# Result stores issued by ScalarE, fewer landing waits on GpSimd's indirect transfers, and separate buffers for the last gathers, in a six-layer attention and mixture-of-experts kernel

## The chip, the cores and the metric

The kernel runs on one core of a Trainium2 chip, in one launch. The metric is the device time of that launch in microseconds (us). The core has TensorE (PE), VectorE (DVE), ScalarE (ACT) and GpSimd (POOL); SyncE (SP) only issues DMAs. ScalarE can issue DMAs too, on a queue of its own. GpSimd issues the indirect ones, which scatter or gather rows by a list of indices.

## The reference

The input is 4096 tokens of 128 numbers (16 batches of 256), and six layers are applied one after another, each to the layernorm of the running sum `x`.

```
x = x + 0.5 * moe0(ln(x))      # 8 experts, top 1, hidden 512, relu squared
x = x + attn0(ln(x))           # latent attention, 8 heads
x = x + 0.5 * moe0(ln(x))
x = x + 0.5 * moe1(ln(x))      # 32 experts, top 4 + a shared expert, hidden 128, silu gate
x = x + attn1(ln(x))           # rotary attention, 16 heads of 8
x = x + 0.5 * moe1(ln(x))
```

In a mixture-of-experts layer each token goes to its K best experts only (K = 1 in moe0, 4 in moe1), and the K outputs are added up with the router's weights.

## The kernel before

Work is ordered by semaphores that are written by hand; each engine runs its own program in order. The names with `rt_`, `dp_`, `bl_`, `cb_` and `sh_` are semaphores. `x` stays in SBUF (`X`), as 32 tiles of 128 tokens; four tiles are a group, so there are 8 groups (0 to 7). Code calls the two kinds of layer `L0` ("top1", moe0) and `L1` ("top4", moe1).

A mixture-of-experts layer has two parts, of 16 tiles each, and these stages:

1. Routing (`route_vector`): VectorE works out for each token and choice a row in a table of slots in HBM, sorted by expert, into `ROW`.
2. Sending (`dispatch_pool`, line 619): GpSimd scatters the normed tokens to `L.xs` (shown as slots_top), one indirect transfer of 128 rows (64 KB) for each tile and choice: 64 for each part in L1, 16 in L0. It waits now and then until all that it has sent has landed (`dp_sent`), in L1 once in 8 transfers in the first part and once in 4 in the second, in L0 never in the first part and once in 4 in the second. Meanwhile PE, ACT and DVE work on the first half of the shared expert (L1 only).
3. Blocks: a step takes four blocks of 128 slots (L1; two in L0), each with its expert's weights. A part has 24 steps in L1 and 12 in L0. SyncE (`blocks_sync`) loads step s+3 (line 764) into one of four buffers `XG` once the transposes of step s are done, and stores the results of step s-2 (L1; s-1 in L0) from one of two buffers `YS` to `L.ys` (results_top, line 768). Step s of PE (`top4_tensor`) is: transposes of step s+1 (line 887), up of s (902), down of s-2 (924), transposes of the hidden values of s-1 (910). ACT copies the transposed inputs (959), applies silu (969) and copies the result of s-2 into `YS` (953), in this order. The first loads wait for the first part's sending, and the load of step 24, part 2's first, waits for all of part 2's sending. So the results of steps 22 and 23 are made only after step 24's load, in PE's steps 24 and 25.
4. Gathering (`combine_pool`, line 1075): when all results of a part are stored (`bl_st`), GpSimd gathers them back, group by group, 16 transfers of 128 rows each in L1 (4 in L0). In L1 group g goes to half g % 2 of a buffer `YG`, once VectorE has combined group g-2 (`cb_add`). It waits for landing after every 4 transfers in groups 0 to 3, and after the first 8 only in groups 4 to 7.
5. Combining (`combine_group`, line 1096): VectorE adds the gathered rows to `X`, groups 0 to 2 between the block steps of part 2 (after its steps 11, 17 and 23), group 3 after them, and groups 4 to 7 in a tail in which PE, ACT and VectorE also do the second half of the shared expert (`TAIL`) and the next layer's layernorm. The shared expert uses the second half of `HF[:, 0]` for a turned copy.

## Time and profile before

| | |
|---|---|
| median of 3 runs | 1943.48 us (1939.62 to 1945.4) |
| profiled execution, its own time | 1943.49 us |
| its span in the trace | 1941.6 us |
| busy: PE, DVE, ACT, POOL | 63%, 58%, 40%, 50% of the span |
| the two moe1 layers in the trace | sending begins at 635.19 and 1506.52 us; the last group's combine begins at 1056.98 and 1927.81 us |

The span runs from the first to the last instruction; 1.9 us of the execution's own time lie around it. Busy shares are averages over stages with different limits. A row of the timeline gives start and length in us, and in brackets how long the engine was idle before it and who ended that; "issue" is time in which it waited for nothing that the profile shows.

### The profile page before, as it was taken

The numbers are of one execution on the slowest core, as the hardware profiler recorded it, in microseconds if no ns is written. First come the engines' busy times: TensorE is split into PE (matmuls) and PEld (weight loads), VectorE is DVE, ScalarE is ACT, GpSimd is POOL, SyncE is SP. The second block draws the span as 40 slices with busy tenths as digits, with TensorE's granted clock in tenths as the row PEclk, the third lists the DMA queues.
The fourth block names the chain that finished last, engine by engine and source line by source line (L and its number), as shares of the span: only waits on it lengthen the run. The fifth ranks groups of instructions, "written<-read, shape, count | busy, mean of one in ns | idle before, by whom it ended". The sixth has DMA issues, their size and how long they took to land.

```text
span 1941.6 us, 34590 instructions
## 1 busy us (share of the span) xinstructions
PE 1223.6 (63%) x11544; PEld 904.9 (47%) x11545; DVE 1135.1 (58%) x2883; ACT 782.2 (40%) x1164; POOL 966.6 (50%) x1052
## 2 busy tenths in 40 slices
PE   2397587862981359779353578777762349678360
PEld 1297355551981128668321244444432129678320
DVE  6546667666468713225357699899978713225332
ACT  2153266650440114334111488788881114334110
POOL 0625145443241665535574467666740665535564
PEclk9998689985995589889776555555555679889785
DMA  8233044401220115345211000000000115345212
GB/s 336 66 96 103 18 155 148 139 15 37 87 82 14 41 46 179 130 137 167 83 49 35 13 2 2 2 2 2 2 2 1 43 58 177 122 147 160 78 49 76
DMA packets 99997, 150.42 MB, mean 77 GB/s; under 512 B 21408, under 2 KB 54816, under 8 KB 99104
## 3 DMA queue, kind: packets, MB, share of 16 engines
q1 hardware_dynamic: 79392, 106.76, 16.7%
q0 software_dynamic: 20480, 41.98, 7.4%
q8 instruction: 79, 1.29, 0.3%
q14 instruction: 46, 0.38, 0.1%
HBM read 74.16 MB, written 74.45 MB: 77 GB/s over the span
## 4 chain that ended last, share of the span: by engine, by line
POOL 24%; PE 23%; issue 16%; DMA 15%; DVE 14%; SPq 5%; ACT 2%; DVEq 0%; ACTq 0%; POOLq 0%
POOL slots_top L619 12%; POOL AREA L1075 11%; DMA slots_top<-XN,ROW 6%; DMA AREA<-results_top,ROW 5%; PE PS L841 4%; SPq L1274 3%; PE PS L293 2%; PE PS L295 2%; PE PS L294 2%; PE PS L1718 2%; DVE AREA L1884 2%; PE PS L1734 2%; PE PS L1706 2%; DMA query_rows<-AREA 1%; PE PS L412 1%
## 5 line engine op out<-in xcount | busy, mean ns | idle before, releaser
L619 POOL DMA_INDIRECT slots_top<-XN,ROW x320 | 315.0, 984 | 363.2 <-DVE ROW L573 183.8
L1075 POOL DMA_INDIRECT AREA<-results_top,ROW x320 | 305.2, 954 | 310.9 <-DMA results_top<-AREA 123.6
L990 DVE SCALAR_TENSOR_TENSOR AREA<-PS,AREA 128x512 f32<-128x512 f32 x96 | 66.4, 691 | 295.5 <-ACT AREA L969 295.0
L1679 POOL TENSOR_TENSOR AREA<-AREA 128x1024 f16<-128x1024 f32 x64 | 151.3, 2364 | 91.1 <-ACT AREA L1819 90.9
L902 PE MATMUL PS<-WGU,AREA 128*128 x768 | 189.5, 391 | 0.0
L1908 DVE TENSOR_REDUCE AREA<-PS 128x4 f32<-128x1024 f32 x128 | 156.0, 1219 | 30.1 <-PE PS L1706 29.3
L1812 ACT ACTIVATE AREA<-PS,AREA 128x1024 f32<-128x1024 f32 x128 | 142.7, 1115 | 52.6 <-PE PS L1718 52.4
L902 PEld LDWEIGHTS PS<-WGU,AREA 128*128 128x128 f32 x768 | 144.0, 198 | 17.1 <-ACT AREA L959 0.4
L1307 POOL TENSOR_TENSOR AREA<-AREA 128x1536 f16<-128x1536 f32 x32 | 92.9, 2904 | 98.4 <-ACT AREA L1522 98.4
L1819 ACT ACTIVATE AREA<-AREA 128x1024 f16<-128x1024 f32 x128 | 135.5, 1059 | 0.0
L412 PE MATMUL PS<-IDF,XN 128*128 128x128 f32 x192 | 50.4, 422 | 135.0 <-DVE XN L402 135.0
L1096 DVE SCALAR_TENSOR_TENSOR X<-AREA,W,X 128x128 f32<-128x128 f32 x256 | 73.2, 348 | 93.3 <-DMA AREA<-results_top,ROW 91.5
L887 PE MATMUL PS<-IDF,AREA 128*128 128x128 f32 x384 | 61.2, 286 | 102.0 <-DMA AREA<-slots_top 102.0
L1734 PEld LDWEIGHTS PS<-AREA 128*128 128x128 f16 x1024 | 63.2, 105 | 124.9 <-issue 84.6
L1734 PE MATMUL PS<-AREA 128*128 (+1 forms) x1024 | 75.2, 179 | 69.3 <-ACT AREA L1840 35.4
L924 PE MATMUL PS<-WD,AREA 128*128 x768 | 103.8, 279 | 12.9 <-DVE AREA L985 12.9
L924 PEld LDWEIGHTS PS<-WD,AREA 128*128 128x128 f32 x768 | 102.0, 194 | 20.3 <-DVE AREA L985 11.8
L959 ACT ACTIVATE AREA<-PS 128x512 f32<-128x512 f32 x96 | 57.3, 597 | 130.3 <-PE PS L887 123.7
L705 ACT ACTIVATE AREA<-PS 128x512 f32<-128x512 f32 x64 | 38.2, 597 | 173.9 <-PE PS L295 173.8
L969 ACT ACTIVATE AREA<-PS 128x512 f32<-128x512 f32 x96 | 57.5, 599 | 122.7 <-PE PS L902 110.9
L412 PEld LDWEIGHTS PS<-IDF,XN 128*128 128x128 f32 x192 | 33.7, 212 | 143.0 <-DVE XN L402 103.0
L1884 DVE TENSOR_TENSOR AREA<-AREA 128x1024 f16<-128x1024 f32 x64 | 97.1, 1517 | 3.4 <-ACT AREA L1819 3.3
(260 smaller groups left out, 3558.9 us busy)
## 6 DMA issues: line engine op xcount, KB each, us to landing
AREA<-slots_top SPq DMA_DIRECT2D x96, 256.0 KB, 3.0
results_top<-AREA SPq DMA_DIRECT2D x96, 256.0 KB, 2.1
slots_top<-ZERO SPq DMA_DIRECT2D x24, 512.0 KB, 3.1
AREA<-slots_top SPq DMA_DIRECT2D x48, 128.0 KB, 2.3
results_top<-AREA SPq DMA_DIRECT2D x48, 128.0 KB, 1.7
AREA<-query_rows SPq DMA_DIRECT2D x48, 128.0 KB, 2.9
slots_top<-XN,ROW POOLq DMA_INDIRECT x320, 2.2
AREA<-results_top,ROW POOLq DMA_INDIRECT x320
```

The source lines that it names most:

```text
L412: ins = nc.tensor.transpose(banks(at + g % 2)[:, j * P:(j + 1) * P], XN[:, t * D:(t + 1) * D], IDF[:, :])
L619: nc.gpsimd.indirect_dma_start(out=L.xs[q], out_offset=bass.IndirectOffsetOnAxis(ap=ROW[:, n:n + 1], axis=0), in_=XN[:, t * D:(t + 1) * D] ...
L902: ins = nc.tensor.matmul(o, XTF[:, v, j * P:(j + 1) * P], w, start=True, stop=True)
L924: ins = nc.tensor.matmul(banks(6 + v)[:, j * D:(j + 1) * D], HF[:, v, 4 * P + j * P:4 * P + (j + 1) * P], w, start=True, stop=True)
L1075: nc.gpsimd.indirect_dma_start(out=YG[:, at:at + D], out_offset=None, in_=L.ys[g * GT // L.tiles], in_offset=bass.IndirectOffsetOnAxis(ap= ...
L1307: nc.gpsimd.tensor_tensor(PB0[1][:, u % 2, :], PF[:, u % 2, :], PB0[0][:, u % 2, :], ALU.subtract).then_inc(a_plo.sem, 1)
L1679: nc.gpsimd.tensor_tensor(PB1[1][:, g, :], PF1[:, g, :], PB1[0][:, g, :], ALU.subtract).then_inc(b_plo[1].sem, 1)
L1734: nc.tensor.matmul(banks(6)[:, o:o + 17], p[0], v, start=k == 0, stop=False)
L1812: nc.scalar.activation(PF1[:, g, :], banks(4, 2), ACT.Exp, bias=LNSP[:, 0:1], scale=SCALE1).then_inc(b_exp.sem, 1)
L1819: nc.scalar.activation(PB1[0][:, g, :], PF1[:, g, :], ACT.Copy).then_inc(b_phi.sem, 1)
L1884: nc.vector.tensor_tensor(PB1[1][:, g, :], PF1[:, g, :], PB1[0][:, g, :], ALU.subtract).then_inc(b_plo[0].sem, 1)
L1908: nc.vector.reduce_max(by_group(MX[:, c % 2, :], g), PS[:, 2:4, :].rearrange("p b (r k) -> p b r k", k=256), axis=AX.X).then_inc(b_max.sem, 1)
```

## The change

It has four pieces. Results are stored from ScalarE's queue, directly behind the copy that makes them (`store_result`), and SyncE only loads. GpSimd's waits for landing in L1 become rarer: once in 16 transfers in the first part of sending and once in 8 in the second, and in gathers of groups 0 to 3 once in 8. In L1 groups 6 and 7 are gathered into the space of `XG` and `HF`, which are free when the blocks are done, in place of the halves of `YG`. The shared expert's turned copy moves from `HF` to `XTF`, so that it doesn't meet group 7. L0 keeps its four buffers and its waits.

```diff
-        self.ring = 4 if K == 1 else 2
+        self.slot = [g % 4 for g in range(NG)] if K == 1 else [0, 1, 0, 1, 0, 1, 2, 3]
+        self.turn = [self.slot[:g].count(u) for g, u in enumerate(self.slot)]
...
+        turned_rows = XTF[:, 0, :]
+        slots = {"top1": [YG[:, u * GT * D:(u + 1) * GT * D] for u in range(4)],
+                 "top4": [YG[:, :GT * 4 * D], YG[:, GT * 4 * D:], XG.rearrange("p a b -> p (a b)"),
+                          HF.rearrange("p a b -> p (a b)")]}
...
-                every = 4 if q > 0 else 8 if L is L1 else 0
+                every = (16, 8)[q] if L is L1 else (0, 4)[q]
                 if every and n % every == every - 1:
                     pool.wait_ge(*dp_sent[q].at(16 * (n % (L.tiles * L.K) + 1)))
...
-                nc.scalar.activation(HF[:, 0, GC:2 * GC], banks(4), ACT.Copy).then_inc(sh_tc.sem, 1)
+                nc.scalar.activation(turned_rows, banks(4), ACT.Copy).then_inc(sh_tc.sem, 1)
...
-                if not is_static(s) or s >= behind:
-                    store(s - behind, (u - behind) % 4)
...
-            for s in range(L.steps - behind, L.steps):
-                store(s, s % 4)
+            sp.wait_ge(*bl_y.at(L.steps))
+
+        def store_result(act, L, s, u, q):
+
+            act.wait_ge(*bl_y.at(s + 1))
+            rows = L.ys[q].rearrange("(n p j) c -> p n (j c)", p=P, j=L.J)
+            nc.scalar.dma_start(rows[:, bass.ds(s - q * L.part_steps, 1), :].rearrange("p a c -> p (a c)"),
+                                YS[:, u % 2, :L.J * D]).then_inc(bl_st[u % 2].sem, 16)
...
                 nc.scalar.activation(YS[:, u % 2, :], banks(6 + u % 2), ACT.Copy).then_inc(bl_y.sem, 1)
+                store_result(act, L, s, u, s // L.part_steps if is_static(s) else part[0])
...
-                u = g % L.ring
-                wait(pool, cb_add[u], g // L.ring)
+                u = L.slot[g]
+                wait(pool, cb_add[u], L.turn[g])
...
-                    if c % 4 == 3 and (g < NG // 2 or c % 8 == 7 and c < GK - 1):
-                        pool.wait_ge(*cb_got[u].at(16 * (g // L.ring * GK + c + 1)))
+                    if c % 8 == 7 and (g < NG // 2 or c < GK - 1) or L is L0 and c == 3 and g < NG // 2:
+                        pool.wait_ge(*cb_got[u].at(16 * (L.turn[g] * GK + c + 1)))
```

GpSimd's program at the end of the second part's sending and the beginning of the gathers of moe1 was this before (a row is a run of equal instructions; what the first of them waits for stands in brackets, and the semaphores are "dispatched", "block_stored", "combine_gathered" and "combine_added"):

```order
L619 DMA slots_top4_1<-XN,ROW 12288x128 [waits dispatched1]
L619 DMA slots_top4_1<-XN,ROW 12288x128 x3
L1075 DMA AREA<-results_top4_0,ROW 128x128 [waits block_stored1,block_stored,dispatched1]
L1075 DMA AREA<-results_top4_0,ROW 128x128 x3
L1075 DMA AREA<-results_top4_0,ROW 128x128 [waits combine_gathered0]
```

The same place in the changed program:

```order
L624 DMA slots_top4_1<-XN,ROW 12288x128 [waits dispatched1]
L624 DMA slots_top4_1<-XN,ROW 12288x128 x7
L1086 DMA AREA<-results_top4_0,ROW 128x128 [waits block_stored1,block_stored,dispatched1]
L1086 DMA AREA<-results_top4_0,ROW 128x128 x7
L1086 DMA AREA<-results_top4_0,ROW 128x128 [waits combine_gathered0]
```

Runs of four became runs of eight, sending and gathering; what the first gather waits for is the same.

The gathers of groups 5 to 7, in GpSimd's program of before:

```order
L1075 DMA AREA<-results_top4_1,ROW 128x128 [waits combine_added1]
L1075 DMA AREA<-results_top4_1,ROW 128x128 x7
L1075 DMA AREA<-results_top4_1,ROW 128x128 [waits combine_gathered1]
L1075 DMA AREA<-results_top4_1,ROW 128x128 x7
L1075 DMA AREA<-results_top4_1,ROW 128x128 [waits combine_added0]
```

And now:

```order
L1086 DMA AREA<-results_top4_1,ROW 128x128 [waits combine_added1]
L1086 DMA AREA<-results_top4_1,ROW 128x128 x7
L1086 DMA AREA<-results_top4_1,ROW 128x128 [waits combine_gathered1]
L1086 DMA AREA<-results_top4_1,ROW 128x128 x15
L1086 DMA AREA<-results_top4_1,ROW 128x128 [waits combine_gathered2]
```

Group 6 follows group 5 with no wait for VectorE's combine of group 4 between them; the wait after eight transfers of a group is still there.

## Rows read from the trace of the kernel before

**Rows 1.** The page: the span, and each engine's busy time, share and instructions.

```profile
span 1941.6 us, 34590 instructions
PE 1223.6 (63%) x11544; PEld 904.9 (47%) x11545; DVE 1135.1 (58%) x2883; ACT 782.2 (40%) x1164; POOL 966.6 (50%) x1052
```

**Rows 2.** The page: the chain that ended last, shares by line.

```profile
POOL slots_top L619 12%; POOL AREA L1075 11%; DMA slots_top<-XN,ROW 6%; DMA AREA<-results_top,ROW 5%; PE PS L841 4%; SPq L1274 3%; PE PS L293 2%; PE PS L295 2%; PE PS L294 2%; PE PS L1718 2%; DVE AREA L1884 2%; PE PS L1734 2%; PE PS L1706 2%; DMA query_rows<-AREA 1%; PE PS L412 1%
```

**Rows 3.** Timeline of GpSimd, first moe1 layer: where its stages begin.

```profile
635.19 1.00 POOL L619 DMA_INDIRECT slots_top<-XN,ROW  x1 [41.25 <-DVE ROW L573]
...
727.40 0.96 POOL L619 DMA_INDIRECT slots_top<-XN,ROW  x1 [1.54 <-DMA slots_top<-XN,ROW]
...
855.30 0.97 POOL L1075 DMA_INDIRECT AREA<-results_top,ROW  x1 [20.40 <-DMA results_top<-AREA]
...
967.18 0.94 POOL L1075 DMA_INDIRECT AREA<-results_top,ROW  x1 [1.81 <-DMA AREA<-results_top,ROW]
```

**Rows 4.** Timeline of SyncE's queue, first moe1 layer: part 2's first load.

```profile
836.19 0.33 SPq L764 DMA_DIRECT2D AREA<-slots_top  x1
836.57 0.43 SPq L768 DMA_DIRECT2D results_top<-AREA  x1
```

**Rows 5.** Timeline of PE, first moe1 layer: the transposes of step 24.

```profile
839.06 1.12 PE L887 MATMUL PS<-IDF,AREA 128*128 128x128 f32 x4 [27.89 <-DMA AREA<-slots_top]
```

**Rows 6.** GpSimd's waits (total us, times, longest): 635:728, 728.5:806, 806.5:836, 856.5:936, 936:968.

```profile
POOL slots_top L619 <- DMA slots_top<-XN,ROW: 12.3, 8, 1.5
...
POOL slots_top L619 <- DMA slots_top<-XN,ROW: 25.4, 11, 2.8
...
POOL slots_top L619 <- DMA slots_top<-XN,ROW: 6.1, 4, 1.5
...
POOL AREA L1075 <- DMA AREA<-results_top,ROW: 27.2, 11, 3.2
...
POOL AREA L1075 <- DMA AREA<-results_top,ROW: 9.1, 5, 1.9
```

**Rows 7.** The same view in the last layer: stretches 1600:1708 and 1727:1838.5.

```profile
POOL slots_top L619 <- DMA slots_top<-XN,ROW: 30.9, 15, 2.9
...
POOL AREA L1075 <- DMA AREA<-results_top,ROW: 36.5, 16, 2.9
```

**Rows 8.** GpSimd's groups of instructions, 727.3:836: busy us, mean ns, idle before.

```profile
L619 POOL DMA_INDIRECT slots_top<-XN,ROW x64 | 61.4, 959 | 47.7 <-DMA slots_top<-XN,ROW 33.1 <-issue 14.6
```

**Rows 9.** Timeline of GpSimd: a stall, and waits behind 20 and 16 transfers.

```profile
63.94 5.49 POOL L619 DMA_INDIRECT slots_top<-XN,ROW  x1 [0.30 <-issue]
...
487.48 0.95 POOL L619 DMA_INDIRECT slots_top<-XN,ROW  x1 [1.79 <-DMA slots_top<-XN,ROW]
...
1000.41 0.94 POOL L1075 DMA_INDIRECT AREA<-results_top,ROW  x1 [1.81 <-DMA AREA<-results_top,ROW]
```

**Rows 10.** Timeline of VectorE: combines of groups 0, 2, 3 and 7, then the last layer's last.

```profile
887.75 4.65 DVE L1096 SCALAR_TENSOR_TENSOR X<-AREA,W,X 128x128 f32<-128x128 f32 x16
...
940.87 4.68 DVE L1096 SCALAR_TENSOR_TENSOR X<-AREA,W,X 128x128 f32<-128x128 f32 x16 [2.94 <-DMA AREA<-results_top,ROW]
945.58 0.87 DVE L366 BATCH_NORM_STATS2 STAT<-X 128x6 f32<-128x128 f32 x4
...
966.94 4.69 DVE L1096 SCALAR_TENSOR_TENSOR X<-AREA,W,X 128x128 f32<-128x128 f32 x16 [20.49 <-DMA AREA<-results_top,ROW]
...
1056.98 4.67 DVE L1096 SCALAR_TENSOR_TENSOR X<-AREA,W,X 128x128 f32<-128x128 f32 x16 [0.87 <-DMA AREA<-results_top,ROW]
...
1927.81 4.66 DVE L1096 SCALAR_TENSOR_TENSOR X<-AREA,W,X 128x128 f32<-128x128 f32 x16 [18.25 <-DMA AREA<-results_top,ROW]
```

**Rows 11.** Timeline of ACT: a step of L0's blocks and one of L1's.

```profile
521.74 1.02 ACT L1021 ACTIVATE AREA<-PS 128x1024 f32<-128x1024 f32 x1 [0.67 <-PE PS L295]
...
854.37 0.60 ACT L969 ACTIVATE AREA<-PS 128x512 f32<-128x512 f32 x1 [1.13 <-PE PS L902]
```

**Rows 12.** The page: a result store of L1, KB each and us to landing.

```profile
results_top<-AREA SPq DMA_DIRECT2D x96, 256.0 KB, 2.1
```

More of the change, by code:

```diff
@@ L660, in turned @@
                 for t in range(GT):
-                    ins = nc.tensor.transpose(banks(7)[:, t * D:(t + 1) * D], HF[:, 0, GC + t * P:GC + (t + 1) * P],
+                    ins = nc.tensor.transpose(banks(7)[:, t * D:(t + 1) * D], turned_rows[:, t * P:(t + 1) * P],
                                               IDF[:, :])
@@ L752, in blocks_sync, with of_step @@
             sp.wait_ge(*dp_sent[0].at(16 * L.tiles * L.K))
-            XC, YC = L.J * D, L.J * D
-            def of_step(parts, s):
+            XC = L.J * D
+            def of_step(s):
                 q = s // L.part_steps if is_static(s) else part[0]
-                rows = parts[q].rearrange("(n p j) c -> p n (j c)", p=P, j=L.J)
+                rows = L.xs[q].rearrange("(n p j) c -> p n (j c)", p=P, j=L.J)
                 return rows[:, bass.ds(s - q * L.part_steps, 1), :].rearrange("p a c -> p (a c)")
             part = [0]
-            behind = 2 if L is L1 else 1
             def load(s, u):
-                sp.dma_start(XG[:, u, :XC], of_step(L.xs, s)).then_inc(bl_load[u].sem, 16)
-            def store(s, u):
-                sp.wait_ge(*bl_y.at(s + 1))
-                sp.dma_start(of_step(L.ys, s), YS[:, u % 2, :YC]).then_inc(bl_st[u % 2].sem, 16)
+                sp.dma_start(XG[:, u, :XC], of_step(s)).then_inc(bl_load[u].sem, 16)
             def step(s, u):
@@ L953, in result @@
                 nc.scalar.activation(YS[:, u % 2, :], banks(6 + u % 2), ACT.Copy).then_inc(bl_y.sem, 1)
+                store_result(act, L, s, u, s // L.part_steps if is_static(s) else part[0])
+            part = [0]
             def x_copy(s, u):
@@ L973, in top4_scalar @@
             x_copy(0, 0)
-            stepped(act, 0, L.steps, step)
+            for q in range(L.parts):
+                part[0] = q
+                stepped(act, q * L.part_steps, (q + 1) * L.part_steps, step)
             result(L.steps - 2, 2)
@@ L1012, in result @@
                                      ).then_inc(bl_y.sem, 1)
+                store_result(act, L, s, u, s // L.part_steps if is_static(s) else part[0])
+            part = [0]
             def step(s, u):
@@ L1025, in blocks_scalar @@
             x_hi(0, 0)
-            stepped(act, 0, L.steps, step)
+            for q in range(L.parts):
+                part[0] = q
+                stepped(act, q * L.part_steps, (q + 1) * L.part_steps, step)
             result(L.steps - 1, 3)
@@ L1070, in combine_pool @@
                         pool.wait_ge(*bl_st[u].at(8 * L.part_steps * (g * GT // L.tiles + 1)))
-                u = g % L.ring
-                wait(pool, cb_add[u], g // L.ring)
+                u = L.slot[g]
+                wait(pool, cb_add[u], L.turn[g])
                 for c in range(GK):
-                    at = (u * GK + c) * D
                     nc.gpsimd.indirect_dma_start(
-                        out=YG[:, at:at + D], out_offset=None, in_=L.ys[g * GT // L.tiles],
+                        out=slots[L.tag][u][:, c * D:(c + 1) * D], out_offset=None, in_=L.ys[g * GT // L.tiles],
                         in_offset=bass.IndirectOffsetOnAxis(ap=ROW[:, g * GK + c:g * GK + c + 1], axis=0)
                     ).then_inc(cb_got[u].sem, 16)
-                    if c % 4 == 3 and (g < NG // 2 or c % 8 == 7 and c < GK - 1):
-                        pool.wait_ge(*cb_got[u].at(16 * (g // L.ring * GK + c + 1)))
+                    if c % 8 == 7 and (g < NG // 2 or c < GK - 1) or L is L0 and c == 3 and g < NG // 2:
+                        pool.wait_ge(*cb_got[u].at(16 * (L.turn[g] * GK + c + 1)))
         def combine_group(dve, L, g, last):
-            u, GK = g % L.ring, GT * L.K
-            dve.wait_ge(*cb_got[u].at((g // L.ring + 1) * (16 * GK)))
-            y = YG[:, u * GK * D:(u + 1) * GK * D]
+            u, GK = L.slot[g], GT * L.K
+            dve.wait_ge(*cb_got[u].at((L.turn[g] + 1) * (16 * GK)))
+            y = slots[L.tag][u]
             if L.K == 1:
@@ L1103, in combine_group @@
             if not last:
-                dve.wait_ge(*cb_add[u].at(g // L.ring + 1))
+                dve.wait_ge(*cb_add[u].at(L.turn[g] + 1))
                 for j in range(GT):
@@ L1958, in moe_counts @@
                 c.update({bl_st[u]: 8 * L.steps})
-            for u in range(L.ring):
-                c.update({cb_got[u]: 16 * GT * L.K * (NG // L.ring), cb_add[u]: NG // L.ring})
+            for u in range(4):
+                c.update({cb_got[u]: 16 * GT * L.K * L.slot.count(u), cb_add[u]: L.slot.count(u)})
             for u in range(4):
@@ L1992, in each_phase @@
                 if ph in ("moe0", "moe1"):
-                    ready = [(cb_add[u].sem, cb_add[u].base) for u in range(2)]
+                    ready = [(cb_add[u].sem, cb_add[u].base) for u in range(4)]
                     if n + 1 < len(phases):
```

## Prediction

> **What bounds the kernel now.** I read the busy times first: no engine is busy for more than 63% of the span, and GpSimd for 50% [rows 1], so the answer lies in who waits for whom. The chain that ended last names GpSimd's sends and gathers for 23% of the span and the landing of just these transfers for 11% more, far ahead of any other line [rows 2]. So I followed GpSimd through the first moe1 layer. It sends part 1 from 635.19 us, part 2 from 727.40, gathers from 855.30, and begins the gathers of group 4 at 967.18 [rows 3]. Each of these beginnings but the gathers' waits only for its own earlier transfers to land. The one at 855.30 waited 20.40 us for result stores. Why: SyncE issues the load of step 24 at 836.19, when part 2's sending has landed [rows 4]; PE had stood still for 27.89 us before it got this data at 839.06 [rows 5]; and the results of steps 22 and 23 need three more steps. So the path is GpSimd's sending, then 855.30 - 836.19 = 19.1 us of blocks, then GpSimd's gathering, and the block work of part 1 and the rest of part 2 lie beside it.
>
> The tail follows. The combine of group 3 begins at 966.94 and that of group 7 at 1056.98, with only 0.87 us of waiting for a gather before it [rows 10], so VectorE's own chain and GpSimd's gathers take the same 90 us there. In the last layer, which prepares no layernorm, the last combine had waited 18.25 us for its gather [rows 10]: there GpSimd alone sets the end.
>
> **The waits for landing.** A send takes 0.96 us and the next begins 0.30 us later; 64 of them take 61.4 + 47.7 us with their waits, of which 14.6 us are the 48 ordinary gaps [rows 8]. A wait for landing stands in place of such a gap, so it costs its length less 0.30. In five stretches [rows 6]:
> - part 1's sending: 12.3 / 8 = 1.54, so 1.24 us each;
> - part 2's sending beside block work: 25.4 / 11 = 2.31, so 2.01 each; after the blocks stopped: 6.1 / 4 = 1.53, so 1.23 each;
> - gathers beside block work: 27.2 / 11 = 2.47, so 2.17 each; after it: 9.1 / 5 = 1.82, so 1.52 each.
>
> The question is whether a wait behind 8 or 16 transfers is longer than one behind 4 or 8. The nearest rows: behind 20 unwaited sends in moe0 the wait was 1.79, behind 16 unwaited gathers 1.81 [rows 9], against 1.53 and 1.82 behind four in quiet stretches. So in quiet it is a latency, paid once whatever the number. Beside block work only waits behind four are shown. I take the same 2.31 and 2.47, as they are 0.77 and 0.65 above the quiet ones, which block traffic explains without a backlog; the other two values are in the rivals.
>
> **The sum, first moe1 layer.**
> 1. Part 1's sending: 8 waits become 4. 4 x 1.24 = 5.0 us. The blocks begin that much earlier, and so does part 2's sending, at 722.4.
> 2. Part 2's sending: the 15 waits inside it become 7, the last landing stays. Eight sends and a wait take 8 x 1.26 + 2.01 = 12.1 us, so the seventh wait ends near 807. Part 1's blocks stop at 839.06 - 27.89 - 5.0 = 806.2, so all seven are beside block work. Gain (11 x 2.01 + 4 x 1.23) - 7 x 2.01 = 13.0 us. Part 2's first load is issued at 836.2 - 18.0 = 818.2; PE still waits for it, some 15 us instead of 27.89, so no new bound appears.
> 3. The gathers then begin 18.0 us earlier, at 837.3. Groups 0 to 3 have 8 waits instead of 16. Eight gathers and a wait take about 8 x 1.25 + 2.17 = 12.2 us; the block part ends 18 us earlier too, which puts six of the waits beside it and two behind. Gain (11 x 2.17 + 5 x 1.52) - (6 x 2.17 + 2 x 1.52) = 31.5 - 16.1 = 15.4 us.
> 4. Group 3's combine can then begin at 966.94 - 33.4 = 933.5. VectorE is ready for it: it was ready for group 2's combine at 940.87 - 2.94 = 937.9, now at 919.9, and with that combine and its statistics done (4.68 + 0.87 us) it is ready for group 3 at 925.5. The buffers hold: group 2's gathers begin near 886, and the combine of group 0, which frees their half, began at 887.75, so now at 869.8, with 4.65 us of work [rows 10].
> 5. The tail keeps its waits (one behind eight transfers in each group), its gathers and VectorE's chain: 0.
> Together 33.4 us.
>
> **Last layer.** The same code and nearly the same rows: 30.9 us for 15 waits where the first has 31.5, and 36.5 for 16 where it has 36.3 [rows 7]. 5.0 + 12.7 + 15.5 = 33.2 us.
>
> **The pieces that I cost at nothing.**
> - Stores on ScalarE's queue. In SyncE's order the store issued at 836.57 stood behind the load that waited for part 2's sending [rows 4], but the next result that would need its buffer is made only behind that load's transposes, so nobody waited. The results of steps 22 and 23, for which the gathers wait, stay bound to step 24. What is added is a wait for ACT's own copy and an issue of 0.33 to 0.43 us [rows 4] in each step, with the input copy and silu (in L0 relu) queued behind. ACT had stood idle for 1.13 us before silu and 0.67 us before relu [rows 11], which covers 0.5. If the cover is gone, an issue costs at most 0.43 on each of 144 steps, 62 us; but blocks are on the path only in L0's two layers (48 steps, 21 us) and for some three steps of each moe1. The Trainium skill says (DMA: Bandwidth & Descriptors, "Issuing engines are not separate DMA queues") that DMAs started by several engines end on the same 16 DMA engines and save only issue time; a gain here would contradict it, and the sum has none.
> - Own rooms for groups 6 and 7. They take away the wait for the combines of groups 4 and 5. The gathers of group 6 begin some 43 us behind 967.18, and group 4's combine is done by then: in the 90 us of the tail GpSimd's stops are for its own landings, as the 1.81 at 1000.41 [rows 9]. 0 us.
> - The turned copy in another place, and two more semaphores at the end: the same instructions, 0.
>
> Sum: 1943.5 - 33.4 - 33.2 = 1876.9 us. It is made against the profiled execution's 1943.49 (span 1941.6, plus 1.9 around it), which is the median of the three runs, 1943.48.
>
> **Rivals.**
> - *Waits grow with what is in flight.* For it: beside block work even four transfers wait longer. If the part above the quiet wait doubles (0.77 for 7 and 0.65 for 6 waits in each layer), 2 x (5.4 + 3.9) = 18.6 us are lost: 1895.5. If the time beside block work stays wholly what it was, what remains is per layer 5.0 + 4 x 1.23 + 3 x 1.52 = 14.5: 1914.5. Against it: the quiet rows behind 16 and 20. Chance 0.19, mostly the first. The Trainium skill speaks for it: DMA: Bandwidth & Descriptors ("Latency and other measured facts") puts HBM's access latency at 0.2 us on average and 2 us at high load; by that each of 26 waits could be 1.8 us longer, an estimate of 47 us and 1924. The rows have shown 0.77 at most.
> - *Waits shrink.* Before, the rhythm of four gathers and a wait (about 7 us) was close to two block steps, so a wait could meet a load each time. With another rhythm all 26 may come down to the quiet ones: 18.6 us more gain, 1858.3. VectorE's readiness (4.) allows some 8 us more per layer, just so much. Chance 0.08.
> - *ACT is held by its DMA.* If ACT's queue stood until a store lands (2.1 us [rows 12]), it would be over its cover by about 1 us per step, mostly off the path in moe1, and add 20 to 50 us: 1900 to 1930. Chance 0.04.
> - *Slower: GpSimd itself stalls when more than eight of its transfers are out.* One send of 640 took 5.49 us in place of 0.96, and it was the ninth of a sequence with no wait [rows 9]. If each of the 4 + 8 + 8 groups of a layer met such a stall once, 40 x 4.5 = 180 us come back: 2057. It decides against the change from 66.6 / 40 = 1.7 us per group on. Against it: the twenty sends before 487.48 and the sixteen gathers before 1000.41 ran with no such stall. Chance 0.03.
> - *No change*: the path's waits are replaced by others, say PE's blocks, to within 0.3%. PE's 27.89 us of standing still speak against it. Chance 0.03.
>
> My forecast with its own range, 1867 to 1887, has 0.63. The range from 1858 to 1900 takes in the shrinking waits and the doubled ones. Faster by over 0.3% (a bound that I take as what a measurement here can tell from no change): 0.94; within it 0.03; slower 0.03.
>
> **What would show it.** In the changed profile: a wait behind 16 sends of about 1.5 us, and four of them; part 2's first load about 183 us behind the first send (201 before); GpSimd's waits beside block work near 2.3 and 2.5 us, half as many; PE's stop before step 24 near 15 us; the first gather about 19 us behind that load, and group 3's combine about 298 us behind the first send (332 before); a tail of 90 us; block steps as long as before. I am wrong if the waits that are left are much longer, if a stall inside a send appears, if block steps become longer with ACT's issues in them, or if VectorE comes late to group 3.

## Result: 1872.1 us for 1941.6, and the opposite on two other chips

Timed beside the kernel before on one chip, the changed kernel took 1872.09 us (median of four runs, 1870.31 to 1873.8), the kernel before 1941.55 (1938.97 to 1945.4). The ratio is 0.9641, with a 95% interval of 0.9625 to 0.9657: faster by 3.6%. The forecast sum of 1876.9 was 4.8 us too high, and the time lies in the narrow range, 1867 to 1887. The experiments below show that this holds for some chips only: on two others the changed kernel and all its variants with rarer waits are 6 to 10% slower than the kernel before (the variant with the old waits: 1.3%). No step of the prediction speaks of that.

The profile's page of the changed kernel: its span, the engines' busy times, and the chain that ended last by engine and by line. Line 619 of before is now 624 (the sends), 1075 is 1086 (the gathers), 1096 is 1107 (the combines).

```profile
span 1872.0 us, 34469 instructions
...
PE 1221.8 (65%) x11513; PEld 902.4 (48%) x11545; DVE 1135.0 (61%) x2883; ACT 785.3 (42%) x1164; POOL 968.9 (52%) x1052
...
PE 33%; POOL 19%; DVE 18%; issue 14%; DMA 8%; SPq 4%; ACT 2%; DVEq 0%; ACTq 0%; another core or an unknown queue 0%; POOLq 0%
POOL slots_top L624 14%; POOL AREA L1086 5%; PE PS L845 4%; PE PS L906 4%; DMA slots_top<-XN,ROW 3%; PE PS L298 3%; SPq L1285 3%; DVE X L1107 3%; PE PS L300 3%; PE PS L299 3%; PE PS L1729 2%; PE PS L928 2%; DVE AREA L1895 2%; PE PS L1745 2%; PE PS L1717 2%
```

Against [rows 1] and [rows 2] no engine's busy time moved by more than about 3 us. What went is waiting: the landing of sends has 3% of the chain where it had 6%, and the landing of gathers, 5% before, is no longer in the list. The chain now goes through PE's blocks and VectorE's combines instead of through GpSimd's gathers, which had 11% and have 5%.

GpSimd's stages in the first moe1 layer, from its timeline (start, duration, then the idle time before and what ended it), beside [rows 3]:

```profile
640.64 1.00 POOL L624 DMA_INDIRECT slots_top<-XN,ROW  x1 [41.26 <-DVE ROW L578]
...
729.21 0.96 POOL L624 DMA_INDIRECT slots_top<-XN,ROW  x1 [1.54 <-DMA slots_top<-XN,ROW]
...
840.26 0.97 POOL L1086 DMA_INDIRECT AREA<-results_top,ROW  x1 [19.57 <-DMA results_top<-AREA]
...
935.56 0.94 POOL L1086 DMA_INDIRECT AREA<-results_top,ROW  x1 [1.89 <-DMA AREA<-results_top,ROW]
```

Part 1's sending takes 88.6 us (92.2 before), part 2's and the blocks behind it 111.1 (127.9), the gathers of groups 0 to 3 95.3 (111.9). From the first send to the first gather it is 199.6 us for 220.1, and to group 4's gathers 294.9 for 332.0.

GpSimd's waits in the stretches 640.6:730, 730:841 and 841:935 of the first moe1 layer and in its tail, 935:1030 (total us, times, longest), beside [rows 6]:

```profile
POOL slots_top L624 <- DMA slots_top<-XN,ROW: 6.2, 4, 1.5
...
POOL slots_top L624 <- DMA slots_top<-XN,ROW: 14.7, 8, 2.5
...
POOL AREA L1086 <- DMA AREA<-results_top,ROW: 13.9, 6, 3.0
POOL AREA L1086 <- DVE X L1107: 2.1, 2, 1.8
...
POOL AREA L1086 <- DMA AREA<-results_top,ROW: 9.4, 5, 1.9
```

Four waits of 1.54 us behind 16 sends each, as forecast. The eight of the second row are the seven inside part 2's sending and once more the 1.54 before it: 13.2 / 7 = 1.88 us where waits behind four sends had been 2.31 beside block work. (In the last layer the seven are 14.3 us, 2.04 each.) Nowhere does a wait show a backlog. The Trainium skill (DMA: Bandwidth & Descriptors, "Latency and other measured facts") puts HBM's access latency at 2 us at high load, which stood behind the estimate of 1924 us. Whether the load here is high in its sense, no run shows; the waits beside block work are on average 0.3 and 0.5 us above the quiet 1.54 in the two layers, not 1.8 (the longest single one is 3.3).

The row for VectorE names no wait for a combine. It holds one gap of 0.30 and this one, the first of the two rows:

```profile
900.42 0.94 POOL L1086 DMA_INDIRECT AREA<-results_top,ROW  x1 [1.77 <-DVE X L1107]
...
911.86 0.94 POOL L1086 DMA_INDIRECT AREA<-results_top,ROW  x1 [1.76 <-DMA AREA<-results_top,ROW]
```

900.42 is the sixth run of eight, the second half of group 2. There GpSimd's program waits for landing only; the wait for group 1's combine stands before group 3, at 911.86. The trace's landing events say the same: the last transfer of the run before landed at 900.17. Group 1's combine happened to end at 895.73 + 4.66 = 900.39, so the view names it. All eight waits of groups 0 to 3 are for landing, 17.5 us together.

PE, SyncE's queue and VectorE at the places of [rows 4], [rows 5] and [rows 10], from their timelines: PE's transposes of step 24, the loads from part 2's first one on, and the combines of groups 1, 3 and 7, and the last layer's last.

```profile
824.65 1.12 PE L891 MATMUL PS<-IDF,AREA 128*128 128x128 f32 x4 [11.85 <-DMA AREA<-slots_top]
...
821.97 4.16 SPq L768 DMA_DIRECT2D AREA<-slots_top  x5
...
895.73 4.66 DVE L1107 SCALAR_TENSOR_TENSOR X<-AREA,W,X 128x128 f32<-128x128 f32 x16
...
935.33 4.68 DVE L1107 SCALAR_TENSOR_TENSOR X<-AREA,W,X 128x128 f32<-128x128 f32 x16 [9.06 <-DMA AREA<-results_top,ROW]
...
1023.59 4.66 DVE L1107 SCALAR_TENSOR_TENSOR X<-AREA,W,X 128x128 f32<-128x128 f32 x16
...
1858.16 4.67 DVE L1107 SCALAR_TENSOR_TENSOR X<-AREA,W,X 128x128 f32<-128x128 f32 x16 [16.28 <-DMA AREA<-results_top,ROW]
```

Group 3's combine comes 935.33 - 640.64 = 294.7 us behind the first send (331.75 before), group 7's 382.95 (421.8). The last combine of this layer no longer waits for its gather: VectorE's chain ends the layer now. (In the last layer it still waits, 16.28 us.)

The tail is 935.33 to 1023.59, 88.3 us, where it was 90.0. In the kernel before GpSimd made one stop there that the changed kernel, with rooms of their own for groups 6 and 7, does not have. It is behind group 7's first gather, and the profile gives no reason:

```profile
1032.17 0.95 POOL L1075 DMA_INDIRECT AREA<-results_top,ROW  x1 [0.30 <-issue]
1035.27 0.95 POOL L1075 DMA_INDIRECT AREA<-results_top,ROW  x1 [2.16 <-issue]
```

And ScalarE, which issues the stores now (L788), in one step of L1's blocks, beside [rows 11]:

```profile
840.15 0.60 ACT L957 ACTIVATE AREA<-PS 128x512 f32<-128x512 f32 x1 [0.29 <-PE PS L928]
840.78 0.34 ACTq L788 DMA_DIRECT2D results_top<-AREA  x1
841.22 0.60 ACT L965 ACTIVATE AREA<-PS 128x512 f32<-128x512 f32 x1 [0.47 <-PE PS L891]
842.75 0.60 ACT L975 ACTIVATE AREA<-PS 128x512 f32<-128x512 f32 x1 [0.94 <-PE PS L906]
843.64 0.60 ACT L957 ACTIVATE AREA<-PS 128x512 f32<-128x512 f32 x1 [0.29 <-PE PS L928]
```

The issue takes 0.34 us and fits into a gap in which ScalarE waits for PE. A step still takes 843.64 - 840.15 = 3.49 us.

Sum over the trace: 1941.6 - 1872.0 = 69.6 us. The first moe1 layer gives 38.8 up to group 7's combine, the last layer, from its first send at 1473.46 (1506.52 before) to the end, 36.5. Ahead of the first moe1, 5.5 us are lost (635.19 against 640.64), mostly in attn0, where nothing was changed. Two later experiments (f1 and f2) with the changed kernel's code up to there begin at 635.92 and 635.28, so it is not the code. Whether the other three executions of the changed kernel had it too is not known: they took 1.6 to 3.5 us less than the profiled one.

### The profile page after: what moved, and what is told of

It is laid out like the page before. It is cut to its first block, busy times and chain, and to the rows that moved or that the text cites. A ratio compares the mean times of both kernels' runs of the same rounds, so it can differ in the third digit from the quotient of the medians.

```text
span 1872.0 us, 34469 instructions
## 1 busy us (share of the span) xinstructions
PE 1221.8 (65%) x11513; PEld 902.4 (48%) x11545; DVE 1135.0 (61%) x2883; ACT 785.3 (42%) x1164; POOL 968.9 (52%) x1052
## 4 chain that ended last, share of the span: by engine, by line
PE 33%; POOL 19%; DVE 18%; issue 14%; DMA 8%; SPq 4%; ACT 2%; DVEq 0%; ACTq 0%; another core or an unknown queue 0%; POOLq 0%
POOL slots_top L624 14%; POOL AREA L1086 5%; PE PS L845 4%; PE PS L906 4%; DMA slots_top<-XN,ROW 3%; PE PS L298 3%; SPq L1285 3%; DVE X L1107 3%; PE PS L300 3%; PE PS L299 3%; PE PS L1729 2%; PE PS L928 2%; DVE AREA L1895 2%; PE PS L1745 2%; PE PS L1717 2%
## 5 line engine op out<-in xcount | busy, mean ns | idle before, releaser
L965 ACT ACTIVATE AREA<-PS 128x512 f32<-128x512 f32 x96 | 57.3, 597 | 131.0 <-PE PS L891 130.3
L710 ACT ACTIVATE AREA<-PS 128x512 f32<-128x512 f32 x64 | 38.2, 597 | 148.5 <-PE PS L300 147.6
L423 ACT ACTIVATE XT<-PS 128x512 f16<-128x512 f32 x48 | 28.7, 597 | 165.9 <-PE PS L417 165.9
```

## Experiments

There are twelve experiments, on four chips: A (e1 to e4), B (c1 to c3 and e5), C (f1 to f3) and D (g1). The kernel before was timed between the others on each chip, and the ratios below are to that. Among the twelve are both kernels unchanged (c1, c2) and one variant twice (e2, c3). The kernel before took 2003.59 us on A, 2006.25 on B, 1940.53 on C and 1941.84 on D. On C and D it has the time of the first comparison.

### First four, on chip A: which part gives the gain?

Theory A was the prediction's, that the waits alone give the gain; theory B that stores and rooms are needed for it. **e1_old_waits** is the changed kernel with the old waits:

```diff
-                every = (16, 8)[q] if L is L1 else (0, 4)[q]
+                every = 4 if q > 0 else 8 if L is L1 else 0
...
-                    if c % 8 == 7 and (g < NG // 2 or c < GK - 1) or L is L0 and c == 3 and g < NG // 2:
+                    if c % 4 == 3 and (g < NG // 2 or c % 8 == 7 and c < GK - 1):
```

> The changed kernel with the landing waits of before (8 and 4 sends, 4 gathers), but with ScalarE's stores and the own rooms kept. Theory A (the whole gain is the removed waits; stores and rooms are worth nothing): the time of before, 1941.5 us, within 4. Theory B (a queue of their own for the stores shortens the waits beside block work, as the profile of the changed kernel has them at 1.9 to 2.0 us in sending and 2.2 in gathering where before had 2.31 and 2.47): 22 waits in each moe1 layer shorter by some 0.35 us, 1926 us.

**e2_waits_only** is the kernel before with the two lines above turned the other way (stores on SP, shared rooms).

> The kernel before with the new, rarer waits alone; stores stay on SyncE's queue, two halves of YG, turned copy in HF. Theory A: the time of the changed kernel, 1872 us, within 4. Theory B: the waits beside block work go back to 2.31 and 2.47 us, 13 of them in each moe1 layer, so 1881 us.

**e3_no_rooms** is the changed kernel with the rooms and the turned copy as before:

```diff
-        self.slot = [g % 4 for g in range(NG)] if K == 1 else [0, 1, 0, 1, 0, 1, 2, 3]
+        self.slot = [g % 4 for g in range(NG)] if K == 1 else [0, 1, 0, 1, 0, 1, 0, 1]
...
-        turned_rows = XTF[:, 0, :]
+        turned_rows = HF[:, 0, GC:2 * GC]
```

> The changed kernel without the own rooms: groups 6 and 7 are gathered into the two halves of YG again and the turned copy is in HF. If the rooms are worth nothing: 1872 us, and no wait of GpSimd for VectorE in the tail. Rival (the rooms gave the tail, which is 1.8 us shorter in the first moe1 layer, its gain): 1875 to 1877 us.

**e4_first_send_8** is the changed kernel with `every = (8, 8)[q]` in place of `(16, 8)[q]`.

> The changed kernel with a wait once in 8 in the first part of sending, as before. Four more waits of 1.54 us in each moe1 layer, each in place of a gap of 0.30: 4 x 1.24 x 2 = 9.9 us more, 1882 us. Rival (the blocks, not GpSimd, set when things go on, so that these waits are hidden): 1872 us.

Measured on A: e1 2030.44 us, 1.0133 (1.0085 to 1.0181); e2 2192.98, 1.0959 (1.0897 to 1.102); e3 2198.34, 1.0991 (1.0935 to 1.1046); e4 2167.84, 1.0828 (1.078 to 1.0876). Theories A and B and the rivals beside them missed: here rare waits make the kernel 8 to 10% slower. The intervals of e2 and e3 overlap, and the two differ in the stores' queue alone, so it makes no difference that shows beside that.

### Next four, on chip B: is it the kernels or the chip?

**c1_after** is the changed kernel itself, **c2_before** the kernel before, **c3_waits_only** is e2 again.

> The changed kernel itself, beside the kernel before on one chip, because the first four experiments ran on a chip on which the kernel before took 2003.6 us instead of 1941.6 and every version with the rare waits was 8 to 10 per cent slower. Theory C (the chip decides: on some chips PE, ScalarE and VectorE stand still while GpSimd's transfers run without pauses): on a chip where the kernel before takes about 1942 us this takes 0.964 of it, as in the first comparison; on one where it takes about 2000 us, 1.08 to 1.10 of it, and the shared expert of the first group ends behind part 2's sending instead of ahead of it. Theory D (the experiments' kernels differ from the changed kernel in something that costs the 9 per cent): 0.964 on either chip.

> The kernel before, for its profile on this chip. Theory C: if its time is about 1942 us, the page is that of the profile before, with the shared expert's first group done about 72 us behind the first sending's start (706.8 for 635.2); if it is about 2000 us, the idle time that no core of this program explains shows on ScalarE and PE during the sendings here too, 30 to 60 us of it, and the rare waits only multiply it. Theory D: no such idle time on any chip.

> The kernel before with the rare waits alone: stores stay on SP's queue and the last gathers in the shared rooms. On the first chip it took 1.0959 of the time before. Theory A (the waits alone give the gain, where the chip lets them): 0.964 to 0.967 on a chip with about 1942 us. Theory B (stores on ScalarE's queue and own rooms are needed, since gathers would then wait for results or rooms): 0.975 to 0.99. On a chip with about 2000 us: 1.08 to 1.10 by theory C.

**e5_gather_4** is the changed kernel with the second edit of e1 alone, the gathers' wait.

> The changed kernel with the wait of the gathers of groups 0 to 3 back at once in 4 transfers. By the prediction's term (3), 15.4 us a layer of the second kind, 30.8 in all: 1903 us, or 0.980 of the time before, on a chip with about 1942 us. Rival: the gathers' gain was already lost to group 3's gathers waiting for the combine of group 1 (3.03, 1.77 and 2.37 us rows of the profile after), so that half of the term at most comes back: 1888 us, 0.972. On a chip with about 2000 us: if the dense gathers are what stalls the other engines, it comes down from 1.09 to 1.04 or less; if it is the sendings, it stays within 1 per cent of the changed kernel.

Measured on B: c1 2174.24 us, 1.084 (1.0794 to 1.0886); c2 2005.01; c3 2149.23, 1.0738 (1.068 to 1.0796); e5 2132.18, 1.0631 (1.0588 to 1.0674). The changed kernel, unchanged, is 8.4% slower than before here. (e5's rival rests on the 1.77 us taken for a wait for a combine; it is one for landing, as shown above.) So it is the chip, or what surrounds it (what else ran near it is not known), and not the experiments' code. The gathers' waits give 2% of the time back (e5, 1.063 for 1.084). With the sendings' waits back too (e1, on A) it is 1.013, so most of the rest goes with the sendings, if A and B are alike. Stores and rooms seem to cost about 1% there: e1 on A is 1.3% slower with the old waits, and c1 is 1% above c3, though their intervals just touch.

Where it goes: the page of c1_after, the chain by engine, then the same row of c2_before.

```profile
PE 33%; DVE 20%; another core or an unknown queue 20%; issue 14%; ACT 4%; SPq 4%; DMA 2%; POOL 1%; ACTq 1%; DVEq 0%; POOLq 0%
```

```profile
PE 22%; issue 19%; DVE 17%; POOL 16%; DMA 13%; another core or an unknown queue 5%; SPq 4%; ACT 3%; DVEq 0%; ACTq 0%; POOLq 0%
```

A fifth of the changed kernel's span is time in which an engine waited and no event in the profile explains its release. The program runs on one core, so the label ("remote" in the views of waits) only means "not known". On the first chip that share was 0%. GpSimd, by contrast, has 1% of the chain. Its stages on B, from the timelines of c1_after and then c2_before: first send and first gather, then the last layer's first send.

```profile
675.66 1.00 POOL L624 DMA_INDIRECT slots_top<-XN,ROW  x1 [43.77 <-DVE ROW L578]
...
952.89 0.97 POOL L1086 DMA_INDIRECT AREA<-results_top,ROW  x1 [99.09 <-DMA results_top<-AREA]
...
1666.44 1.04 POOL L624 DMA_INDIRECT slots_top<-XN,ROW  x1 [53.16 <-DVE ROW L578]
```

```profile
671.29 1.00 POOL L619 DMA_INDIRECT slots_top<-XN,ROW  x1 [44.03 <-DVE ROW L573]
...
891.97 0.97 POOL L1075 DMA_INDIRECT AREA<-results_top,ROW  x1 [19.45 <-DMA results_top<-AREA]
...
1561.86 1.04 POOL L619 DMA_INDIRECT slots_top<-XN,ROW  x1 [53.18 <-DVE ROW L573]
```

From first send to first gather it is 277.2 us against 220.7, and from there to the next moe1 713.6 against 669.9. GpSimd itself sends without being held up (part 1 takes 89.0 us, 88.6 on the first chip), and then stands still for 99 us, waiting for result stores of blocks that come late. Its landing waits while sending (677:850 in c1_after; total, times, longest) are all quiet ones:

```profile
POOL slots_top L624 <- DMA slots_top<-XN,ROW: 16.9, 11, 1.5
```

The others are late. First ScalarE's waits for its silu of the shared expert in c1_after (620:960, the same columns), then PE, ScalarE and VectorE at one such place, from their timelines:

```profile
ACT AREA L710 <- remote: 117.6, 10, 27.4
```

```profile
754.12 0.63 PE L300 MATMUL PS<-XT,SU 128*128 128x512 f16 x1
...
778.65 0.60 ACT L710 ACTIVATE AREA<-PS 128x512 f32<-128x512 f32 x1 [27.42 <-remote]
...
779.27 0.69 DVE L740 SCALAR_TENSOR_TENSOR AREA<-PS,AREA 128x512 f32<-128x512 f32 x1 [27.32 <-ACT AREA L710]
...
779.78 1.11 PE L666 MATMUL PS<-IDF,AREA 128*128 128x128 f32 x4 [25.03 <-issue]
```

PE's last product for this silu ended at 754.75 by the trace; ScalarE, whose other condition (VectorE's product before) had long been met, began at 778.65, 23.9 us late. VectorE followed as soon as ScalarE was done (0.02 us), and so did PE, which needed ScalarE's next copy (779.14 to 779.73). In the changed kernel on the first chip the same hand-over takes 0.03 us (PE ended at 678.67, ScalarE began at 678.70). So it is the hand-over from PE that comes late. Whether PE tells of its end late, or ScalarE learns of it or acts late, the trace does not say. Ten such waits, 117.6 us together, stand in the first moe1, all begun while GpSimd sends; the two before this one were late by 8.5 us (PE ended at 735.12, ScalarE began at 743.63) and 2.9 us (747.75, 750.63). PE's products are slower there too, 0.63 us for 0.38 on the first chip: the granted clock is 0.64 in 728:755 of c1_after and 0.95 in 674:680 of the first trace. That is PE at the lower of its two levels (1.2 and 2.4 GHz) after it has stood still, and 0.25 us a product does not explain a gap of 23.9. How late the shared expert's first half becomes (its last ScalarE instruction, counted from the first send) goes with the waits:

```
kernel, chip              waits in sendings   last ScalarE instr.   first gather
before, first chip        1 in 8 and 4         +70.3 us             +220.1 us
c2_before, B              1 in 8 and 4         +75.9                +220.7
e1_old_waits, A           1 in 8 and 4         +85.9                +217.9
e4_first_send_8, A        1 in 8 and 8         +83.5                +259.5
e2_waits_only, A          1 in 16 and 8       +189.9                +284.4
c1_after, B               1 in 16 and 8       +181.5                +277.2
after, first chip         1 in 16 and 8        +70.4                +199.6
f2_lagged, C              no pause             +70.4                +183.0
```

On A and B, with one wait in 16 the shared expert lasts until far into part 2's sending. PE's program has part 1's blocks behind it, and 24 steps of 3.49 us are 84 us by this estimate: 181.5 + 84 is 265 of c1's 277.2. With one wait in 8 (e4) the shared expert is done in time, and then the blocks beside part 2's sending are held up instead (ScalarE's silu there has five such waits, 33.2 us). I first thought of instruction fetches that starve behind GpSimd's transfers. Between 690.4 and 855 us of c1_after the instruction queues moved 4 packets, and there are eleven waits of ScalarE and two of VectorE of this kind. That does not fit, and no run here tests it further. The kernel before suffers too, less: 5% of 2003 us is 100 us with no event, and ScalarE's silu of the shared expert alone has 81.8 us of such waits in the two moe1 layers, more than the 30 to 60 of theory C. Yet its sending stage is as long as on the first chip (220.7 for 220.1). Of the 62 us that it is longer on B, 36 lie ahead of the first moe1 layer (671.29 for 635.19), where ScalarE's relu of moe0 has twelve such waits, 47.3 us.

### Three on chip C: pause, or number of transfers out?

Theory E says that GpSimd's pauses are what lets the others go on, theory F that the number of transfers out is what counts. **f1_second_send_4** has `every = (16, 4)[q]`.

> The changed kernel with one wait back: the second sending waits once in 4 transfers as before (first sending once in 16, gathers once in 8). On a chip on which the kernel before takes about 1942 us: seven waits of 1.88 us come back a layer, 13 us, 26 in all, so 1898 us, 0.978. On a chip with about 2005 us: theory E (the other engines are held up while GpSimd's transfers follow each other without a pause, and the second sending is the stretch where it counts, because the shared expert's first half lies beside it) 1.02 to 1.04; rival (the first sending or the gathers are what counts, the second sending does not): 1.07 to 1.08.

**f2_lagged** waits in both sendings of L1, but for a batch of four that is already old. Two semaphores take turns, so that the wait is exact:

```diff
-                    in_=XN[:, t * D:(t + 1) * D], in_offset=None).then_inc(dp_sent[q].sem, 16)
-                every = (16, 8)[q] if L is L1 else (0, 4)[q]
-                if every and n % every == every - 1:
-                    pool.wait_ge(*dp_sent[q].at(16 * (n % (L.tiles * L.K) + 1)))
+                    in_=XN[:, t * D:(t + 1) * D], in_offset=None).then_inc(
+                        (dp_odd if L is L1 and n // 4 % 2 else dp_sent)[q].sem, 16)
+                m = n % (L.tiles * L.K)
+                if L is L0 and q and m % 4 == 3:
+                    pool.wait_ge(*dp_sent[q].at(16 * (m + 1)))
+                if L is L1 and m % 4 == 3 and m > 3:
+                    b = m // 4 - 1
+                    pool.wait_ge(*(dp_odd if b % 2 else dp_sent)[q].at(64 * (b // 2 + 1)))
```

> The changed kernel, but in both sendings GpSimd waits once in 4 transfers for the four before the last four, which have landed by then (5 us back, where a landing takes 2 to 3): so the number of transfers out is held to eight, and there is no pause. Theory E (the pause is what lets the other engines go on): on a chip with about 2005 us it is as slow as the changed kernel or slower, 1.08 to 1.12. Theory F (the number of transfers out is what counts): 1.02 to 1.04. On a chip with about 1942 us both say faster than the changed kernel, as four waits of 1.24 and seven of 1.6 us beyond the normal gap go from each of two layers: 1840 us, 0.948; not below 1855, 0.956, if the blocks of part 2 come before the landing of its last transfers as the bound.

**f3_pause** puts a pause without a landing wait where a wait was dropped (IDLE is a scratch tile):

```diff
+                elif L is L1 and n % (8, 4)[q] == (8, 4)[q] - 1:
+                    for i in range(8):
+                        ins = nc.gpsimd.tensor_tensor(IDLE[0:1, i:i + 1], HALFNEG[0:1, 0:1], HALFNEG[0:1, 0:1],
+                                                      ALU.add)
+                    ins.then_inc(idled.sem, 1)
+                    idle_count[0] += 1
+                    pool.wait_ge(*idled.at(idle_count[0]))
```

> The changed kernel with GpSimd pausing without a wait for landing: where the first sending waited once in 8 and the second once in 4 before, and no longer does, it now does eight one-element operations of its own and waits for them, 1.0 to 1.5 us by the 0.12 us pitch of such operations in attn1. On a chip with about 2005 us: theory E 1.02 to 1.05 (gathers stay rare); theory F 1.08, as nothing waits for landings. On a chip with about 1942 us: twelve such pauses a layer, 12 to 18 us, 1896 to 1908 us by either, 0.977 to 0.983.

Measured on C: f1 1895.42 us, 0.9759 (0.9742 to 0.9776); f2 1833.76, 0.9445 (0.9429 to 0.9461); f3 1903.22, 0.9802 (0.9776 to 0.9828). C is a chip like the first, so E and F were not told apart. They do price the sendings. f1 returns (0.9759 - 0.9641) x 1941 = 23 us, 11.5 a layer, for eight waits put back (seven in the expectation). By its trace the first gather comes 16.1 and 13.7 us later behind the first send in the two layers, more than the time says; the profiled execution of f1 was 5.8 us longer than f1's median, that of the changed kernel 1.7 longer than its own. f1 settles one more thing: it stores from ScalarE's queue, and its fifteen waits in part 2's sending take 30.8 us, as in the kernel before (31.5 and 30.9). So the stores' queue does not shorten these waits. f3 returns 31 us for 24 pauses, 1.3 us each. In its trace 22 of them last 1.50 us, 1.20 beyond an ordinary gap (the first of each layer 3.7): a pause of GpSimd's own costs what a quiet landing wait costs, 1.24. And f2 takes another 38 us away, 16.6 and 18.3 of it up to the first gather (183.0 us for 199.6 in the first layer). GpSimd's waits in its two sendings (637:818) are then only ordinary gaps:

```profile
POOL slots_top L625 <- issue: 38.7, 127, 0.3
```

f2 went below my floor of 1855 us (0.956), for which the blocks should have become the bound. The transposes of its steps, on PE's timeline, run through the place where PE had stood still for 11.85 us:

```profile
801.00 0.60 PE L903 MATMUL PS<-IDF,AREA 128*128 128x128 f32 x4
...
804.49 0.60 PE L903 MATMUL PS<-IDF,AREA 128*128 128x128 f32 x4
```

SyncE's first load of part 2 is issued at 800.75, between two steps at the usual 3.49 us: sending and blocks now end together. So the floor was set too high. That a faster sending would gain nothing more is to be expected from these rows, but no run tests it.

### Last one, on chip D: stores and rooms alone

**g1_lagged_old_stores** is f2 with stores on SP's queue and shared rooms, as before the change.

> The kernel before with the gathers' rare waits (once in 8) and the sendings' lagged waits, but with its stores on SP's queue and the last gathers in the shared rooms: against the lagged version before this one it undoes stores and rooms alone. On a chip on which the kernel before takes about 1942 us: if stores and rooms are worth nothing, as the prediction costed them, 0.9445 of it, within the interval of 0.943 to 0.946; rival, worth something because the last gathers must wait for rooms or the loads stand behind stores in SP's queue: 0.950 or more. On a chip with about 2005 us, beside the 1.0738 of the rare waits alone: theory E (the missing pause holds up the other engines) 1.07 or more, theory F (the number of transfers out does) 1.04 or less.

Measured: 1833.1 us (five runs), 0.9448 (0.9429 to 0.9466), f2's 0.9445 again. Stores, rooms and turned copy are worth nothing that the time shows on these chips, at least with these waits. The traces do show something for the rooms: from group 3's combine to group 7's it is 87.9 and 88.2 us in f2, 89.9 and 90.1 in g1, which has the stop behind group 7's first gather again. That is 1.9 us a layer, about what the expectation of e3 had as its rival; a difference of 3.9 us lies within the two intervals, some 3 us to either side each. g1 and f2 beat both kernels, on chips like the first. On chips like A and B they were not tried.

## Why the prediction was right, and where it was not

- **Bound and path.** Right. GpSimd's sending, some 19 us of blocks (821.97 to 840.26 is 18.3) and its gathering set the time, and what they lost the layer lost: 38.8 us of the first moe1 layer, for 33.4 forecast.
- **Term 1, part 1's sending, 5.0 us.** Four waits of 1.54 us are as forecast. The stage gave 3.6, as the 64 sends themselves took 64.1 us in place of 62.9: behind the eighth some take up to 1.66 us instead of 0.96. The same sends are long in every kernel that waits once in 16 or only for old batches, and 0.96 again with a wait or a pause after eight (e1, e4, f3).
- **Term 2, 13.0 us, load 183 us behind the first send.** It came at 821.97 - 640.64 = 181.3. With term 1 the sum was 18.0, measured 19.7, so this term gave 16.1. The surplus of 3 is the waits, 1.88 us for an assumed 2.31: a part of the rival "waits shrink". Why they are shorter no run shows; with four sends to a wait they are 2.3 in f1 as before. PE's stop was 11.85 us, "some 15" forecast. f1, with the opposite edit, prices the term at 11.5 us a layer in time and 13.7 to 16.1 in the trace.
- **Term 3, 15.4 us.** Measured 16.6. The eight waits are 17.5 us, where six of 2.47 and two of 1.82 are 18.5. None was for a combine. The prediction had worked out that the buffer is free in time for group 2's gathers only; for group 3's it is too, as group 1's combine ends at 900.39 and they begin at 911.86. No run on a chip like the first puts the gathers' waits back alone (e5 met chip B), so this term is shown by the trace and not by an experiment.
- **Term 4, VectorE ready at group 3.** Right: its combine still had 9.06 us to wait, so the whole gain went through.
- **Term 5, tail of 90 us.** 1023.59 - 935.33 = 88.3. The term was put at 0 and measured 1.8: the prediction read GpSimd's stops in the tail as waits for its own landings, and missed the stop of 2.16 us that goes with the shared rooms. The bound changed as well: in the first moe1 layer the last combine waits no more for its gather.
- **Last layer, 33.2 us.** 36.5 in the trace: 17.5 up to the first gather, 17.0 in the gathers of groups 0 to 3, 2.0 in the tail.
- **The number.** The two layers gave 38.84 + 36.54 = 75.4 us in the trace, 8.8 more than the 66.6 forecast. The profiled execution lost 5.8 us elsewhere, most of it in attn0. That the time came within 4.8 us of the forecast is in part this accident, and errors of opposite sign in terms 1 and 2 are another.
- **Pieces at nothing.** Stores on ScalarE's queue: 0.34 us under ScalarE's own waits, step length unchanged, f2 and g1 equal. The rooms are the exception, 1.9 us a layer (term 5). The Trainium skill says (DMA: Bandwidth & Descriptors, "Issuing engines are not separate DMA queues") that DMAs started by several engines interleave on the same 16 DMA engines and save only issue time. The runs agree: f1's waits beside the stores of ScalarE's queue are as long as before (30.8 us for 31.5 and 30.9), and no time came of it.
- **Rivals.** Longer waits and a ScalarE held by its DMA did not occur on chips like the first. Neither did the stall of GpSimd in the size feared: in moe1 no send of any run is longer than 1.82 us, and the one of 5.49 us of [rows 9] is there in every kernel at the same place, the ninth send of the first layer (of 320; with the gathers there are 640 transfers). In small the rival was true, as term 1 shows.
- **What failed.** The chance of 0.03 for "slower" rested on one mechanism, a stall of GpSimd of 1.7 us or more in each group of transfers. On A and B the kernel is slower by another one: GpSimd's sends go on as before, and the engines beside it stand still. The prediction took the block work and the shared expert to run at their own pace whatever GpSimd does. That is so on the first chip, C and D, not on A and B. The trace of before could not show it, as it came from a chip where this is true: on which kind of chip the comparison would be made was luck.

What stays open: why PE's hand-overs come late beside GpSimd's transfers on A and B. That landing waits while sending keep their 1.5 us there speaks against the number of transfers out; but the two versions made to decide, f2 and f3, met a chip without the effect.

## What to carry to other kernels

A wait for landing that only limits how far an engine runs ahead should ask for an older batch, on chips like the first: two semaphores in turn took away the changed kernel's 22 waits in the sendings (1.8 us on average, 1.5 beyond an ordinary gap), where rarer waits had only halved their number. On chips like A and B this was not tried, and might do harm there. Price such a wait at its length less the ordinary gap, and check that what it releases (here VectorE and the halves of the buffer) can come earlier. And time a change of this kind on more than one chip: before one believes a gain, and before one explains it, both kernels, unchanged, should be timed beside the experiments on the same chip.

## What the runs showed of the hardware that was not expected

- Chips (or what surrounds them) differ for the same kernel by almost as much as the change is worth, 62 to 66 us for 69.5: the kernel before took 2003.6 and 2006.3 us on two of them and 1940.5 to 1941.8 in the other comparisons. And a change can have the opposite sign: the changed kernel took 1.084 times the time before on B, 0.964 on the first.
- On B a hand-over from PE to ScalarE took up to 23.9 us while GpSimd issued indirect transfers every 1.26 us, and 0.03 us on the first chip. GpSimd's own waits for landing in part 1's sending were 1.54 us on both. The cause is open.
- A landing wait behind 16 sends is no longer than one behind four (1.54 us), and beside block work waits behind eight (1.88, and 2.04 in the last layer) were shorter than those behind four had been (2.31).
- GpSimd issued 64 sends in a row, and 64 more, with no pause but 0.3 us gaps (f2). Of these, none is longer than 1.68 us; the eighth, which is as long (1.67 us) in every kernel, and a few behind it (the ninth, and two near the eighteenth) take 1.43 to 1.68 in place of 0.96. Those behind it do not where GpSimd waits or pauses after eight.
- With the last two groups gathered into shared rooms, GpSimd stops for 2.1 us behind the first gather of group 7, with no event in the profile; with rooms of their own it does not (f2 against g1, and the two kernels).
